# A two-layer decoder on one core: expert combine, preparation and state scan put into one block, with dt and dt·u of the second channel tile behind the first scan

## The reference, cut to what matters

```
y = jnp.sum(outs * topk_weight[..., None], axis=1)          # 4 expert rows for each token
x = x + y                                                   # "combine"
# state-space block, on layernorm(x):
xn = x * rsqrt(mean(x*x) + EPS) * norm_w
x_inner, z = split(einsum('bld,ed->ble', xn, in_proj_w))    # 512 + 512 channels
xc = silu(causal_conv4(x_inner) + conv_b)
x_ssm = einsum('bld,ed->ble', xc, x_proj_w)                 # B (16), C (16), dt (1)
dt = softplus(x_ssm[..., -1:] * dt_w[:, 0] + dt_b)
h = exp(dt * A) * h + (dt * u) * B                          # scan over 128 steps, 16 states
y = sum(h * C) + D_param * u
out = einsum('ble,de->bld', y * silu(z), out_proj_w) + residual
# later: bitlinear158 weights  clip(round(w * scale), -1, 1),  scale = 1 / mean(|w|)
```

## Time and profile before

| | us |
|---|---|
| median of 3 runs (lowest, highest) | 957.99 (953.48, 958.64) |
| the profiled execution, its own time | 956.03 |
| span of its trace | 954.3 |
| expert stage and the barrier behind it | 409 to 538 |
| combine | 538 to 584.1 |
| preparation | 584.1 to 650.5 |
| scan stage | 650.5 to 826.3 |
| recurrence and feed-forward | 826.3 to 954.3 |

### The profile page before, as it was taken

The page is one execution under the profiler, slowest core; times in us unless marked ns, Lnnn a source line. Parts: engine busy times, 40 slices in busy tenths (PEclk is TensorE's granted clock), DMA queues, the critical chain, the costliest instruction groups (busy, mean ns, idle before and its releaser), DMA issues. The chain is left out here.

```text
span 954.3 us, 14595 instructions
## 1 busy us (share of the span) xinstructions
PE 761.9 (80%) x4329; PEld 545.7 (57%) x4329; DVE 738.7 (77%) x1554; ACT 531.3 (56%) x1352; POOL 502.5 (53%) x529
## 2 busy tenths in 40 slices
PE   6788999999999988369999425786999999950265
PEld 2467888888888776257777212244555555540133
DVE  1484878888888886767777457885999999779876
ACT  0223455655655665246666422679788788218185
POOL 1001767777777775055554372314899788523210
PEclk9779999999999999679999757896999999995577
DMA  8804400000000130035547452003233223010000
GB/s 283 288 0 183 172 1 2 1 7 1 7 7 1 52 145 12 7 88 144 147 150 137 132 192 74 1 3 133 72 105 110 86 91 111 1 44 0 1 17 28
DMA packets 30189, 72.45 MB, mean 76 GB/s; under 512 B 5649, under 2 KB 19729, under 8 KB 27617
## 3 DMA queue, kind: packets, MB, share of 16 engines
q1 hardware_dynamic: 25504, 58.93, 17.6%
q0 software_dynamic: 4608, 12.59, 5.5%
HBM read 60.96 MB, written 10.55 MB: 75 GB/s over the span
## 5 line engine op out<-in xcount | busy, mean ns | idle before, releaser
L1746 POOL TENSOR_TENSOR arena<-arena 128x1024 f32<-128x1024 f32 x63 | 147.6, 2374 | 30.6 <-DVE arena L1712 30.6
L1712 DVE TENSOR_TENSOR_SCAN arena<-arena,ps 128x1024 f32<-128x1024 f32 x64 | 143.5, 2276 | 13.4 <-PE ps L1633 8.5
L1653 PE MATMUL ps<-arena 128*128 128x512 f32 x256 | 120.1, 592 | 0.0
L811 ACT ACTIVATE arena<-arena 128x128 f32<-128x128 f32 x256 | 98.9, 390 | 12.3 <-DVE arena L735 12.2
L614 PE MATMUL ps<-arena 128*128 128x128 f32 (+1 forms) x768 | 101.4, 283 | 0.8 <-PEq L345 0.8
L614 PEld LDWEIGHTS ps<-arena 128*128 128x128 f32 (+1 forms) x768 | 92.3, 195 | 13.9 <-issue 12.3
L1037 POOL DMA_INDIRECT arena<-tokens,arena x64 | 62.1, 971 | 67.1 <-PE ps L1058 50.2
L819 ACT ACTIVATE arena<-ps 128x512 f32<-128x512 f32 x64 | 38.2, 597 | 88.0 <-PE ps L633 88.0
L1678 ACT ACTIVATE arena<-arena 128x1016 f32<-128x1016 f32 x64 | 72.5, 1135 | 22.7 <-DVE arena L1712 22.6
L1688 ACT ACTIVATE arena<-arena 128x256 f32<-128x256 f32 x192 | 81.3, 494 | 0.1
L862 POOL TENSOR_TENSOR arena<-arena 128x512 f32<-128x512 f32 x64 | 66.7, 1042 | 20.7 <-DVE arena L741 20.7
(11 more groups left out here) (315 smaller groups left out, 1658.3 us busy)
## 6 DMA issues: line engine op xcount, KB each, us to landing
arena<-c_rows SPq DMA_DIRECT2D x32, 512.0 KB, 3.6
arena<-in_E_gu SPq DMA_DIRECT2D x8, 1024.0 KB, 12.1
expert_out<-arena SPq DMA_DIRECT2D x64, 128.0 KB, 2.3
arena<-in_E_dn SPq DMA_DIRECT2D x1, 4096.0 KB, 12.2
arena<-in_ctxT SPq DMA_DIRECT2D x2, 1024.0 KB, 5.0
arena<-in_X_o SPq DMA_DIRECT2D x1, 2048.0 KB, 19.6
arena<-in_A_o SPq DMA_DIRECT2D x1, 2048.0 KB, 26.7
arena<-in_F_w SPq DMA_DIRECT2D x2, 1024.0 KB, 5.0
```

The source lines that it names most:

```text
L811: t = eng.activation(pr[:, i % 3, j, :], sm[:, d, j, :], ACT.Exp, bias=negm[:, d, j:j + 1], scale=SCALE[slots[i][0]], accum_out=rsum[:, i ...
L1653: t = eng.matmul(ps[:, 2 * k + half, :], ident, hC[s % 4][:, half * 512:(half + 1) * 512], start=False, stop=n == ST - 1)
L1712: eng.tensor_tensor_scan(hst[s % 4], dA[s % 4], psD[s % 2].rearrange("p k m -> p (k m)"), 0.0, ALU.mult, ALU.add).then_inc(h_ready, 1)
L1746: eng.tensor_tensor(hC[s % 4], hst[s % 4], Csb[i % 4], ALU.mult).then_inc(hC_ready, 1)
```

## The change

Combine, preparation and scan become one block, so the two barriers between them are gone. The order within each engine's list is new, and the preparation is done in halves of 512 tokens (`half(v, k)`).

- `w1`, `w2`, `vecs`, `w_in`, `w_bc`, `w_out` (3.9 MB in all by their sizes) are loaded by SyncE in the expert block, behind `spread_step` and ahead of the 64 writes of `ys`. Some routing tensors move to other addresses for that.
- The gathers go to a ring of four token tiles; from the fifth tile on GpSimd waits until VectorE has combined the tile four before.
- The ternary weights stand before and behind the first combined tile; the convolution of the first token half stands between the combined tiles of the second half.
- The fourth channel tile's convolution becomes four matmuls with diagonal matrices (`diagW`); these and `diagD` are built by ScalarE.
- dt is now column 97 of the B/C projection, spread over 128 partitions by a matmul with ones (`dt_rows`); ScalarE takes Abs straight from PSUM (`magnitudes`).
- The residual and the split go from VectorE to GpSimd; the square root of the second norm half becomes a power on GpSimd.
- dt and dt·u of channel tile 0 stand before the first scan, of tile 1 behind it, of tiles 2 and 3 behind the second scan. The transposes of dt·u, their copies and the Silu of the second half of z stand inside the scan.

The diff, cut to what the text speaks of:

```diff
@@ expert block, sync
+                eng.wait_ge(spread_step, 2)
+                load(eng, "w1", w1, a["F_w1"])
+                load(eng, "w2", w2, a["F_w2"])
+                load(eng, "vecs", vecs, a["M_vec"])
+                load(eng, "w_in", w_in, a["M_in"])
+                load(eng, "w_bc", w_bc, a["M_bc"])
+                load(eng, "w_out", w_out, a["M_out"])
@@ one block, vector
+                def dt_and_dtu(c):
+                    eng.wait_ge(ln_dt, c + 1)
+                    eng.scalar_tensor_tensor(dts[:, c], dts[:, c], 0.0, dtu[:, c], ALU.max, ALU.add).then_inc(dt_ready, 1)
+                    eng.wait_ge(dt_ready, c + 1)
+                    eng.tensor_tensor(dtu[:, c], dts[:, c], xc[:, c], ALU.mult).then_inc(dtu_ready, 1)
...
+                eng.wait_ge(wsum_done, 1)
...
+                ternary(eng, cw_, 0, w1, w1q)
+                combine(0)
+                ternary(eng, cw_, 1, w2, w2q)
+                for b in range(1, HB):
+                    combine(b)
+                normS.dve_variance(eng, 0)
+                scales_in(eng, cs, 0)
+                scales_out(eng, cs, 0)
+                combine(HB)
+                for c in range(CT - 1):
+                    conv(c, 0)
+                    combine(HB + 1 + c)
+                normS.dve_variance(eng, 1)
+                scales_in(eng, cs, 1)
+                scales_out(eng, cs, 1)
+                steps(0)
+                for c in range(CT - 1):
+                    conv(c, 1)
...
+                steps(1)
...
-                eng.wait_ge(c_stored, 16)
+                dt_and_dtu(0)
+                eng.wait_ge(c_stored, 32)
                 for s in range(SLOTS):
+                    if s == 1:
+                        dt_and_dtu(1)
...
                     scan(s)
+                    if s == 1:
+                        dt_and_dtu(2)
+                        dt_and_dtu(3)
@@ one block, scalar
+                for n in range(CT):
+                    conv_silu(n, 0)
+                bc_rows(0)
+                normS.act(eng, nw, pairs=(2, 4))
+                magnitudes(0)
+                for n in range(CT):
+                    xi(n, 1)
+                exponentials(0)
...
+                    conv_silu(n, 1)
+                for m in (0, 1):
+                    eng.wait_ge(z_done, CT + m + 1)
+                    eng.activation(half(zs[:, m], 1), ps[:, Z_BANK[1][m], :], ACT.Copy).then_inc(z_moved, 1)
+                bc_rows(1)
+                magnitudes(1)
+                exponentials(1)
+                eng.wait_ge(exp_ready, 2 * CT)
+                for c in range(CT):
+                    eng.activation(dtu[:, c], dtu[:, c], ACT.Ln, bias=1.0).then_inc(ln_dt, 1)
...
                     scaled(i, 0, NB // 2)
                     decay(2 * i)
+                    if i in (0, 2):
+                        turned_dtu(i)
                     scaled(i, NB // 2, NB)
                     decay(2 * i + 1)
+                    if i in (0, 2):
+                        turned_dtu(i + 1)
+                    if i == ST // 2:
...
+                        eng.activation(zs[:, :, HT:], zs[:, :, HT:], ACT.Silu).then_inc(zs_ready, 1)
@@ one block, tensor
+                    if s == 2:
+                        turn_dtu(2)
+                        turn_dtu(3)
```

More of the change, by code:

```diff
@@ L77, in decoder @@
         ps = ctx.enter_context(nc.psum_tensor("ps", [P, 8, 512], fp32))
+        loads = {n: [sem("ld_" + n), 0] for n in ("w1", "w2", "vecs", "w_in", "w_bc", "w_out")}
         first_layer = ExitStack()
@@ new lines, in _ @@
+                for b in range(NB):
+                    rows = slice((b % 4) * E, (b % 4 + 1) * E)
+                    t = eng.matmul(ps[:, b, 0:D], weightT[rows, b // 4], bias_dn[rows],
+                                   start=True, stop=True)
+                    if b % 2:
+                        t.then_inc(bias_done, 1)
+                eng.wait_ge(wab_ready, 2)
+                eng.wait_ge(s_comb, NB // 2)
+                eng.matmul(ps[:, 3, 300:302], ones, wab, start=True, stop=True).then_inc(wsum_done, 1)
@@ new lines, in bc_rows, with magnitudes @@
+                def bc_rows(k):
+                    eng.wait_ge(proj_done, k + 1)
+                    eng.activation(half(bcf[0:3 * E + 1], k), ps[0:3 * E + 1, PROJ_BANK[k], :],
+                                   ACT.Copy).then_inc(bcf_ready, 1)
+                def magnitudes(k):
+                    eng.wait_ge(dt_done, k + 1)
+                    for c in range(CT):
+                        eng.activation(half(dtu[:, c], k), ps[:, k, :], ACT.Abs, bias=dtb[:, c:c + 1],
+                                       scale=dtw[:, c:c + 1]).then_inc(abs_ready, 1)
@@ new lines, in exponentials @@
+                def exponentials(k):
+                    eng.wait_ge(abs_ready, CT * (k + 1))
+                    for c in range(CT):
+                        eng.activation(half(dtu[:, c], k), half(dtu[:, c], k), ACT.Exp, scale=-1.0).then_inc(exp_ready, 1)
+                scales_root(eng, 0)
+                normS.act(eng, nw, pairs=(0, 2))
+                for n in range(CT):
+                    xi(n, 0)
+                for m in range(CT):
+                    eng.wait_ge(z_done, m + 1)
+                    eng.activation(half(zs[:, m], 0), ps[:, Z_BANK[0][m], :], ACT.Silu).then_inc(z_ready, 1)
```

558 lines of the change are left out of this document (266 added, 292 removed).

## The result

The changed kernel takes 960.88 us (median of 20 executions, 956.84 to 962.21) where the kernel before takes 956.28 (20 executions, 953.30 to 959.34). The ratio is 1.004, with a 95% interval of 1.0027 to 1.0054. Two repeats of the unaltered changed kernel gave 1.0019 and 1.0054. So it is slower by some 0.2 to 0.5% (the interval of one repeat still holds 1.000), and a gain of 12.5 us was forecast. The time is outside the range of 932 to 954.

The account below looks back on a forecast made before the run. It took engines waiting in turn to bound the work before the first scan, and VectorE the scan. Terms -21.5 (first scan) + 5.7 + 2.0 (scan) + 1.3 (expert stage) = -12.5 on 956.03 gave 943.5 us; range 932 to 954.

Parts of the forecast that it names:

- First scan, 91 us after the block's start: Way from the block's start to the first scan: near 91 us where it was 112.6, a gain of 21.5 us.
- ScalarE's `hT` is done within the same 3.45, at 594.3: Second half before the scan: transposed copies of `h` ready 3.45 us after `h` starts at 590.9.
- matmul 0.5: Chain from the last convolution to the first scan: a TensorE step behind Silu, priced at 0.5 us.
- Its 16 matmuls averaged 0.555 us there: First half's projection on TensorE: 1.7 us taken for the first tile's two matmuls at the lower clock level.
- The second half's convolutions beside GpSimd's residual, +4.5: Before the first scan: VectorE's convolutions stretched by GpSimd's residual and split running beside them, 4.5 us lost.
- The first rival: GpSimd's work stays out of VectorE's way before the scan and the Silu hides: -19 us, 937; chance 0.22.
- 80% of 6.0: VectorE's loss as a share of its 6.0 us overlap with GpSimd before the scan: 5.0, taken as 4.5.
- The scan's start, +5.7: First scans: dt and dt·u pairs and turned copies moved behind the first scan put scan 6 at 26.5 us, +5.7.
- It ends at 2.3, dt and dt·u of tile 1 at 4.7: Scan's start on VectorE, from the first scan at 0: first scan over at 2.3 us, tile 1's pair at 4.7.
- Silu and two table loads in the scan, +2.0: At state 8 of the scan ScalarE does 4.5 us of Silu and table loads, of which 2.0 come through.
- Expert stage, +1.3: Weight loads delay the first `ys` row's write to 429.6 where its buffer is wanted at 428.3: 1.3 us lost.
- The third rival: Slower than before: the loads keep the expert stage's writes waiting, +24 us in place of +1.3, 966; chance 0.06.

Follow-up runs that it names:

- again: The changed kernel timed once more, unaltered; 958.77 us, ratio to the kernel before 0.9997 to 1.0040.
- z_first: Changed kernel with the first half's z projections ahead of the fourth convolution tile in TensorE's list; 949.11 us.
- hold: Changed kernel with GpSimd's first two products with C waiting for dt·u, so that none lies beside a dt·u; 954.37 us.
- two_first: Changed kernel with dt and dt·u of tile 1 also ahead of the first scan, behind those of tile 0; 950.56 us.
- pairs_first: Changed kernel with dt and dt·u of all four tiles ahead of the first scan; 956.97 us.
- z_two: Changed kernel with z projections ahead of the fourth convolution tile and dt and dt·u of tile 1 ahead of the first scan; 940.68 us.

## Why the prediction was wrong

The reading that the engines wait in turn before the first scan and that VectorE bounds the scan holds. Its three large terms went as follows.

**First scan, 91 us after the block's start: it was 106.5.** Step by step, predicted and measured: VectorE's first convolution at 34.5 and 37.0; `h` of the second half at 52.9 and 56.2; `steps(0)` at 58.7 and 73.2; first scan at 91.0 and 106.5. The step that failed is the one between `h` and `steps(0)`: "ScalarE's `hT` is done within the same 3.45, at 594.3". It took the gap of 3.45 from a place where TensorE was idle; it was 14.35 (593.29 to 607.64). From `h` to `steps(0)` 5.8 us were forecast and 17.1 came. Here TensorE's list held 6.21 + 7.03 + 3.67 + 1.09 us of work and 1.8 of hand-offs ahead of the second half's transposes (585.62 to 605.37), and all of it stood behind the wait of 6.86 for the fourth copy. I had never priced that list. Of the 11.3 us missed in this step, 4.2 are the list alone, as the profile of again shows (10.0 from `h` to `steps(0)`), and 7.1 are the standing time and the matmuls at the lower clock behind it. z_first shows both: with one piece of the list moved, `steps(0)` came 11.4 us earlier than in the changed kernel's profile and 4.3 earlier than in that of again. Without standing time the first scan would still have missed by 9.6 (100.6 against 91.0): 3.2 up to `h`, 4.2 in this step and 2.2 behind it.

From `steps(0)` on 32.3 were forecast and 33.3 came, and that is luck. The forecast has 4.5 for GpSimd's residual in it, of which 0.8 came; the other 27.8 were 32.5. The same fault is in them: "matmul 0.5" is the whole B, C and dt projection of 3.60 us (L1388, 624.18), which stands in TensorE's list behind two z projections.

Two more errors fed it. "Its 16 matmuls averaged 0.555 us there" was taken to mean 16 matmuls. A projection of one tile with 512 columns is two matmuls, and each float32 matmul leaves two records: four records are a tile, which is 1.72 us at the higher level of the clock, as the copies 1.72 apart show. I priced a projection on TensorE at half of what it takes, so the first convolution came 2.5 us late, and I never saw that TensorE's list could be the longest. And TensorE's signals beside the gathers came so late that ScalarE stood for 4.5 to 7.9 us in most profiles. No row of before could show this: its first half's projection ran beside gathers too (L1268), but no engine waited for one of its tiles.

**The second half's convolutions beside GpSimd's residual, +4.5: it was 0.8.** Three passes of 512 tokens took 2.63, 2.52 and 2.33 us, where in the first half they took 2.33 each, and the shorter first pass up to 0.72 in place of 0.55:

```profile
613.99 2.63 DVE L1662 SCALAR_TENSOR_TENSOR arena<-arena 128x512 f32<-128x512 f32 x3
...
617.30 2.52 DVE L1662 SCALAR_TENSOR_TENSOR arena<-arena 128x512 f32<-128x512 f32 x3
...
620.31 2.33 DVE L1662 SCALAR_TENSOR_TENSOR arena<-arena 128x512 f32<-128x512 f32 x3
...
L1803 POOL TENSOR_SCALAR arena<-arena x8: 1212/1244/1728, 595.4 to 617.6; 128x256 f32<-128x256 f32 x8
```

The first rival was nearly right here, a saving too small to show beside the 15.5 us. The Trainium skill's rule on the shared port (page "SBUF — State Buffer", section "Who interferes with whom"), by which all of the overlap would be lost, does not hold here: seven residual tiles (L1803, 609.35 to 619.16) lie beside the convolutions from 613.24 on, 5.9 us, and VectorE lost 0.8. GpSimd lost more: its tiles went from 1.21 us to 1.73, 1.72 and 1.53, so 1.4. That the overlap is 5.9 where 6.0 were forecast is luck: the convolutions began 13.8 us later than forecast, and the residual, held up by the split's wait for the B and C rows, ended 13.8 later. My "80% of 6.0" came from GpSimd products of two tensors; the residual reads one tensor. That this is the difference was not tried by itself.

**The scan's start, +5.7: it was +11.2, and the scan +11.9 in all.** "It ends at 2.3, dt and dt·u of tile 1 at 4.7" took 1.225 for dt·u. Two of them took 3.25 beside GpSimd's products (hold: 2.8 us of the scan). I had used exactly this collision for the convolution, where it did little, and had forgotten it here. Without it, in hold, the scan is 9.1 over before, where the whole forecast was 7.7; so it is the larger part of the 4.2 that were missed. That most of these 9.1 is the fill of the pipe behind the held-back second slot is what two_first and pairs_first speak for: they get 7.0 and 9.8 of the 11.9 back. For this pair of operations the Trainium skill's rule (page "SBUF — State Buffer", section "Who interferes with whom") and the traces agree: beside a product of 2.37 alone, 2.03 were lost each time.

**Silu and two table loads in the scan, +2.0: 0.7 came through.** The profile after has the load at 697.46 (1.28 us), Silu 1.91, a load at 702.28, and scans 6 to 63 took 153.3 us where they took 152.6 before; the difference lies between scans 19 and 22. No load had a drain beside its 1.28: for these two and the five between 617 us and the first scan, ScalarE's instruction before ends and the one behind starts within 0.02 us of the load.

**Expert stage, +1.3: it was about that.** From the first expert gather to the first gather of the combine, the kernel before needs 129.55 us in its one profile, the changed one 130.2, and the thirteen profiles with its loads 130.9 on average (130.2 to 131.8). The third rival (966 by starving the expert stage) did not occur. The time came out at 961 by another way.

The sum closes. The forecast meant a span of 941.8. Add 15.5 for the first scan and 4.2 for the scan, and take off 2.1 because the block began 0.85 us earlier than before and not 1.3 later: 959.4, and the profiled span is 959.1. This is bookkeeping of one profile, and checks the readings, not the causes.

The range was too narrow for one reason above all: its ends came from prices of work, and the largest error was in an order and in a wait that the order exposed.

## What to carry to other kernels

When a chain is moved forward, write out the in-order list of every engine that it crosses, with the prices of what stands ahead in it, and not only the gaps between the chain's own steps: of the 14.5 us by which `steps(0)` was late, 11.3 lay in one such list and the wait in it. A wait in such a list can cost more than its length: behind 6.86 us of idle time TensorE's next tile took 6.21 us in place of 3.6. Move a piece that only feeds a pipe's second slot ahead of the first if it costs less than the pipe's fill behind it (here 2.4 us for 7.0), and keep the rest behind. Between two versions that each gain, look whether a stall can be covered by work that the engine must do anyway; z_two does it and is 1.3 to 1.8% faster than the kernel before.

## What the runs showed of the hardware

A dt·u of 128x1024 float32 on VectorE takes 1.22 us alone and 3.25 beside a GpSimd product of 2.37, which grows to 3.25 itself.

ScalarE's copies out of PSUM stood for 4.5 to 7.9 us in 9 of 11 profiles in which GpSimd's indirect gathers ran beside them, and in none of two without them. What came late was TensorE's signal of a finished projection; the copies began 0.02 to 0.03 us behind the late ones that the trace has. In four profiles two such signals came 0.06 to 0.08 us apart, for projections of 1.72 us each. The cause stays open.

In the changed kernel's profile TensorE's granted clock fell from 1.00 to 0.50 near the end of 6.86 us in which it stood idle, and the eight matmul records behind took 6.21 us; with hardly a wait before them they take 3.6 to 3.7.

Profiles of kernels that are alike up to the block have it begin between 533.8 and 539.2 us.
